# The row term of the cross attention scores: VectorE multiply-and-sum in place of one-column TensorE products

## The reference, cut to what matters

```python
h = _layernorm(x)                      # the normalised row
q = h @ Wq + bq
k_tok, v_tok = h @ Wk + bk, h @ Wv + bv
k_ext, v_ext = ctx @ Wk + bk, ctx @ Wv + bv
s_self = jnp.einsum('bsh,bsh->bs', q, k_tok)[..., None]
s_ext = jnp.einsum('bsh,beh->bse', q, k_ext)
probs = softmax(concatenate([s_self, s_ext], axis=-1))
out = probs[..., :1] * v_tok + jnp.einsum('bse,beh->bsh', probs[..., 1:], v_ext)
x = x + out
```

## Time and profile before

| | |
|---|---|
| median of three runs | 2739.05 us |
| span of the profiled execution | 2732.5 us |
| median less span | 6.55 us |
| TensorE matmuls, busy | 2354.2 us, 86% |
| VectorE, busy | 1869.3 us, 68% |
| ScalarE, busy | 1643.3 us, 60% |
| GpSimd, busy | 1352.9 us, 50% |

### The profile page before, as it was taken

The page is one execution under the profiler, slowest core; times in us unless marked ns, Lnnn a source line. Parts: engine busy times, 40 slices in busy tenths (PEclk is TensorE's granted clock), DMA queues, the critical chain, the costliest instruction groups (busy, mean ns, idle before and its releaser), DMA issues. The chain is left out here.

```text
span 2732.5 us, 49486 instructions
## 1 busy us (share of the span) xinstructions
PE 2354.2 (86%) x16048; PEld 1842.8 (67%) x16048; DVE 1869.3 (68%) x4490; ACT 1643.3 (60%) x3283; POOL 1352.9 (50%) x1313
## 2 busy tenths in 40 slices
PE   5999999669999958999999999986999898599881
PEld 3667676559999835565665656654787777599881
DVE  3888888545656437777777777772777777477783
ACT  3777777545555426776766767663444343388883
POOL 4777777453334255455454545521556565202556
PEclk9999999779999978999999999996999999799996
DMA  2222222152222001111111111113233433355896
GB/s 62 73 67 74 70 71 66 40 168 73 86 65 66 18 29 32 42 39 43 41 41 42 38 42 39 33 39 127 86 117 121 137 124 107 128 160 181 275 279 199
DMA packets 236524, 241.65 MB, mean 88 GB/s; under 512 B 36926, under 2 KB 222528, under 8 KB 236144
## 3 DMA queue, kind: packets, MB, share of 16 engines
q1 hardware_dynamic: 214704, 192.11, 23.0%
q0 software_dynamic: 20480, 46.39, 5.3%
q10 hardware_dynamic: 1088, 0.00, 0.0%
HBM read 132.78 MB, written 101.25 MB: 86 GB/s over the span
## 5 line engine op out<-in xcount | busy, mean ns | idle before, releaser
L1554 DVE TENSOR_REDUCE f_nm<-f_raw 128x4 f32<-128x1024 f32 x256 | 312.8, 1222 | 107.5 <-PE f_raw L1667 104.6
L1390 POOL TENSOR_TENSOR f_hm<-f_hm,f_mhalf 128x64 f32<-128x64 f32 x32 | 366.4, 11449 | 2.7
L1459 ACT ACTIVATE f_PT<-f_sco 128x1024 f32<-128x1024 f32 x256 | 262.2, 1024 | 99.1 <-PE f_sco L1684 98.7
L2399 POOL DMA_INDIRECT d_pick<-expert_out,e_out_slots x128 | 133.2, 1041 | 221.7 <-DMA expert_out<-d_eo 135.7
L916 ACT ACTIVATE b_hT<-b_H,b_b1r 128x512 f32<-128x512 f32 x128 | 88.4, 691 | 162.4 <-PE b_H L1046 147.0
L1684 PE MATMUL f_sco<-f_q4T,f_k4T 64*128 64x256 f32 x1024 | 130.9, 336 | 51.0 <-DMA f_q4T<-f_nmT 36.6
L1925 POOL DMA_INDIRECT expert_in<-g_xm,e_slots x128 | 129.8, 1014 | 40.2 <-issue 37.0
L677 PE MATMUL a_bank<-a_w,a_xnT 128*128 128x512 f32 x256 | 127.1, 621 | 21.9 <-ACT a_xnT L394 21.9
L1061 PE MATMUL b_O<-b_w2l,b_hTh 128*128 128x256 f32 x512 | 145.9, 285 | 0.0
L1061 PE MATMUL b_O<-b_w2h,b_hTh 128*128 128x256 f32 x512 | 144.7, 283 | 0.0
L1061 PE MATMUL b_O<-b_w2h,b_hTl 128*128 128x256 f32 x512 | 143.6, 280 | 0.0
(11 more groups left out here) (368 smaller groups left out, 7722.3 us busy)
## 6 DMA issues: line engine op xcount, KB each, us to landing
e_xs<-expert_in SPq DMA_DIRECT2D x85, 256.0 KB, 3.3
expert_out<-d_eo SPq DMA_DIRECT2D x85, 256.0 KB, 2.5
x_scratch<-a_x SPq DMA_DIRECT2D x64, 256.0 KB, 3.1
b_w<-in_L_ffn_W_dram SPq DMA_DIRECT2D x16, 1024.0 KB, 5.7
a_x<-in_x_dram SPq DMA_DIRECT2D x32, 256.0 KB, 3.8
a_cx<-in_ctx_dram SPq DMA_DIRECT2D x32, 256.0 KB, 3.4
f_x<-x_scratch SPq DMA_DIRECT2D x32, 256.0 KB, 2.7
f_q4T<-f_nmT SPq DMA_DIRECT2D x128, 64.0 KB, 2.3
```

The costliest lines, as they stand in the source:

```text
L1390: g.tensor_tensor(hm[b % 2][:, :], hm[b % 2][:, :], mhalf[:, :], ALU.pow).then_inc(hroot, 1)
L1459: s.activation(PT[n % 3][:, t, :, :], heads(SCO), ACT.Exp, scale=float(DH) ** -0.5).then_inc(probs_ready, 1)
L1554: v.tensor_reduce(nm[:, t, g * HG:(g + 1) * HG], heads(RAW), AX.X, ALU.max, negate=True)\
L2399: g.indirect_dma_start(pick[b % GR][:, t, c, :], None, ex.eo_d[k], bass.IndirectOffsetOnAxis(ap=ex.out_slots[:, b, t, c:c + 1], axis=0), b ...
```

## The change

The row term is no longer a TensorE product. A new VectorE part, "pre r" (`row_term`), multiplies the normalised row by `wr`, now held as a full row of 256 values on every partition, and sums the product over the columns by the accumulator output of the instruction; it does so once per tile, one round ahead of its use, between "mix mix" and "sco exp". Its result has two buffers. `score_max` reads it there and adds bq·bk inside the two small steps, so the two L2033 instructions go. One wait (`r2_ready`) is added ahead of the first small step, and waits for `xn_ready` and the previous `r2_ready` ahead of the new part. In the attention pass `wr` is made by two 256-column products in place of four one-column ones, and its copy is 256 columns wide instead of 2.

```diff
-        self.wqk, self.g0, self.wr, self.r0 = ..., sb("wr", [P, C]), sb("r0", [P, 1])
+        self.wqk, self.g0, self.wr, self.r0 = ..., sb("wr", [P, D]), sb("r0", [P, 1])
...
-                s.activation(w.wr[:, :], Y[:, C:2 * C], ACT.Copy).then_inc(pro_sb, 1)
+                s.activation(w.wr[:, :], halves(Y)[:, 1, :], ACT.Copy).then_inc(pro_sb, 1)
...
-                    for c in range(C):
-                        t_.matmul(Y[:, C + m:C + m + 1], wqT[:, c, cols], w.bkT[:, c:c + 1], start=c == 0, stop=c == C - 1)
+                for c in range(C):
+                    t_.matmul(halves(Y)[:, 1, :], w.bkT[:, c:c + 1].broadcast_to([P, P]), wqT[:, c, :],
+                              start=c == 0, stop=c == C - 1)
...
-            "mix mix", "sco exp", "pre T", ...
+            "mix mix", "pre r", "sco exp", "pre T", ...
...
                 for t, bank in enumerate((S0, S1)):
                     v.tensor_reduce(m2[:, t:t + 1], bank[:, 0:S + 1], AX.X, ALU.max).then_inc(gate_step, 1)
-                    v.tensor_scalar(r2[:, t:t + 1], bank[:, S + 2:S + 3], r0[:, 0:1], None, ALU.add).then_inc(gate_step, 1)
-                small[0] += 4
+                small[0] += 2
                 dve.wait_ge(gate_step, small[0])
-                v.tensor_tensor(m2[:, :], m2[:, :], r2[:, :], ALU.add).then_inc(gate_step, 1)
+                dve.wait_ge(r2_ready, b + 1)
+                v.scalar_tensor_tensor(m2[:, :], r2[b % 2][:, :], r0[:, 0:1], m2[:, :], ALU.add, ALU.add).then_inc(gate_step, 1)
                 small[0] += 1
                 dve.wait_ge(gate_step, small[0])
-                v.tensor_tensor(nb2[:, :], r2[:, :], m2[:, :], ALU.subtract).then_inc(nb2_ready, 1)
+                v.scalar_tensor_tensor(nb2[:, :], r2[b % 2][:, :], r0[:, 0:1], m2[:, :], ALU.add, ALU.subtract)\
+                    .then_inc(nb2_ready, 1)
+
+            def row_term(b):
+                dve.wait_ge(xn_ready, b + 1)
+                if b:
+                    dve.wait_ge(r2_ready, b)
+                for t in range(T):
+                    last = v.scalar_tensor_tensor(r2_terms[:, t, :], xn[b % 2][:, t, :], 1.0, wr[:, :], ALU.mult, ALU.mult,
+                                                  accum_out=r2[b % 2][:, t:t + 1])
+                last.then_inc(r2_ready, 1)
...
-                for t, bank in enumerate((S0, S1)):
-                    for c in range(C):
-                        t_.matmul(bank[:, S + 2:S + 3], xnT[b % 2][:, c, t * P:(t + 1) * P], wr[:, c:c + 1],
-                                  start=c == 0, stop=c == C - 1)
                 pe.wait_ge(gx_ready, b + 1)
```

More of the change, by code:

```diff
@@ L1090, in __init__ @@
         self.wq_in = [sb("wq_in0", [P, C, D]), sb("wq_in1", [P, C, D])]
-        self.wqk, self.g0, self.wr, self.r0 = sb("wqk", [P, C, D]), sb("g0", [P, C]), sb("wr", [P, C]), sb("r0", [P, 1])
+        self.wqk, self.g0, self.wr, self.r0 = sb("wqk", [P, C, D]), sb("g0", [P, C]), sb("wr", [P, D]), sb("r0", [P, 1])
         self.count = 14
@@ L1756, in cross_pass @@
         pe2, peT = sb("pe2", [P, T, S + 1]), sbn("peT", 2, [P, T, S])
-        m2, nb2, r2 = sb("m2", [P, T]), sb("nb2", [P, T]), sb("r2", [P, T])
+        m2, nb2 = sb("m2", [P, T]), sb("nb2", [P, T])
+        r2, r2_terms = sbn("r2", 2, [P, T]), sb("r2_terms", [P, T, D])
         den2, rden2 = sb("den2", [P, T]), sbn("rden2", 2, [P, T])
@@ L1783, in cross_pass @@
         g_psum, g_ready, gx_step, gx_ready = sem("g_psum"), sem("g_ready"), sem("gx_step"), sem("gx_ready")
+        r2_ready = sem("r2_ready")
         s2_psum, nb2_ready, p2_ready, inverted, own_ready = [sem(n) for n in ("s2_psum", "nb2_ready", "p2_ready", "inverted", "own_ready")]
@@ L1800, in cross_pass @@
             "sco gx", "pre stats", "pre cxT", "gate norm", "part0 high", "sco scores", "gate T", "file rows", "pre norm",
-            "mix mix", "sco exp", "pre T", "sco expT", "mix T", "gate logits", "mix cross", "pre g", "part1 low", "gate ranks")
+            "mix mix", "pre r", "sco exp", "pre T", "sco expT", "mix T", "gate logits", "mix cross", "pre g", "part1 low", "gate ranks")
         PIECES, FIRST = 2 * NE, B // 4
@@ L2178, in _ @@
             slots({"part1 low": split_weights,
-                   "pre stats": stats, "pre norm": norm, "sco scores": score_max, "sco expT": invert, "mix mix": add_mix,
+                   "pre stats": stats, "pre norm": norm, "pre r": row_term, "sco scores": score_max, "sco expT": invert, "mix mix": add_mix,
                    "mix cross": add_cross, "gate norm": norm3, "gate logits": gates, "gate ranks": queue})
```

## The result

The changed kernel takes 2747.01 us (median of 12 runs, 2740.58 to 2756.32) against 2740.02 (12 runs beside it, 2725.05 to 2743.43): ratio 1.0034, 95% interval [1.0018, 1.0051]. A ratio is always that of a kernel to the kernel before, measured beside it, and the brackets behind it are its 95% interval. The forecast was 2732.0 us in a range of 2725 to 2745. The kernel became slower: the difference is small, but the interval lies above 1. The profiled spans go the same way: 2732.5 before, 2748.9 after.

A forecast was written before the change was run, and what follows sets the result against it. GpSimd's chain up to the own score, then VectorE's from the maximum, was taken to bound the cross-pass round. Net 0.22 us over 32 batches saves 7.0 us: span 2725.5, plus 6.55 gives 2732.0 us, range 2725 to 2745.

The forecast's parts named there:

- The folded weights: Making the wider wr, once: eight one-column matmuls become four of 256 columns, the copy grows; below 1 us, taken as 0.
- Rival 3: Cross pass: idle time ahead of the own score drops TensorE's clock, 1.1 us a drop; about 2750 us, chance 0.10.
- The products go: Cross pass, TensorE ahead of the own score: 8 loads, 1.08 us a round, become about 0.92 us idle; gain 0.
- Two small VectorE instructions go: Cross pass, score_max: first maximum to bias falls from 1.24 to 0.99 us, saving 0.25 us a round.
- I cost that at 0: score_max's two small steps becoming scalar-tensor-tensor forms on two columns: no added cost, each still 0.16 us.
- the extra wait: Ahead of score_max's first small step: already fulfilled, handling costs 0.03 us a round (bounds 0 and 0.11).
- Does the rest follow?: Cross pass behind score_max: TensorE's 0.47 us wait ahead of the mix transposes lets the round shorten by the whole 0.22 us.
- The new VectorE part: Cross pass, two multiply-and-sum instructions: 1.1 us (0.88 to 1.35) fits in 1.60 us of room, cost 0.
- The extra wait at its upper bound: Rival "same": the added score_max wait costs 0.11 us, leaving 0 to 4 us gain; about 2737 us, chance 0.30.
- TensorE as the bound: Cross pass: removing the products saves 1.08 us a round, 35 us in all; about 2697 us, chance 0.02.
- Idle takes the clock: Cross pass: 1.3 us without matmuls drops TensorE's clock, 1.1 us a drop; about 2750 us, chance 0.10.
- Row term not hidden: Cross pass: the new VectorE pair takes 2.76 us against 1.60 of room; about 2769 us, chance 0.05.

The follow-up runs named there:

- e1: The changed kernel with 32 unused bytes per partition behind wr (1024 in all); 2728.11 us, ratio 0.997 to the kernel before.
- e2: The kernel before with 992 unused bytes per partition behind wr, no instruction changed; 2759.4 us, ratio 1.0098.
- e16: The kernel before with 32 unused bytes behind wr, and 96 ahead of and 32 behind q4T and nmT each; ratio 1.0001.
- e14: The kernel before with 64 unused bytes per partition behind wr; 2744.6 us, ratio 1.0025.
- e15: The kernel before with 128 unused bytes per partition behind wr; ratio 1.0016.
- e18: The changed kernel with 32 unused bytes ahead of nmT alone and 224 behind it; 2730.72 us, ratio 0.9976 to the kernel before.
- e8: e1 with the removed one-column products put back on TensorE, their result unused; 2731.01 us, ratio 0.998 to the kernel before.
- e17: The kernel before with 32 unused bytes ahead of q4T and 96 behind it; ratio 1.006.
- e7: e1 with bq·bk added a round early by its own instruction, and plain two-operand steps in score_max; 2730.98 us, ratio 0.9968 to the kernel before.
- e11: e1 with GpSimd's indirect DMAs made to wait until the normalised row is written; 2732.31 us, ratio 0.9979 to the kernel before.
- e10: e1 with both the early bq·bk of e7 and the DMA wait of e11; 2725.24 us, ratio 0.9956 to the kernel before.
- e9: e1 with the row term made three times, the extra sums unused; 2739.77 us, ratio 1.0004 to the kernel before.

## Why the prediction was wrong

*The folded weights* is the step that failed: "Both ways below 1 us in all; I take 0". I priced the instructions that make the wider `wr` and not the tile itself. It stands early in the allocation, and its 992 bytes took nmT off a multiple of 256 in another pass. By the ratios this is 1.0034 - 0.997 = 0.64% of 2739, about 17.5 us; between the profiles of after and e1 it is 24.0 us of attention pass. To the kernel before the same 992 bytes cost 1.0% (e2). Neither my range nor a rival held it. Rival 3 names nearly the measured time (2750), but that is luck: it was wrong about how, since the granted clock of the cross pass is 0.95 after and 0.93 before.

How the 24 us come about: from the sixth round on, 0.27 us more in each of 26 rounds (26.2 for 25.9 us undisturbed) is about 7 us; 0.25 of the 0.27 are TensorE's longer wait. In the same rounds 22 instead of 12 hold a stretch at half clock, of 1.1 us each: 10 x 1.1 = 11 us. The first rounds give 3 us more and the end of the pass nearly 4. That the longer wait brings the stretches at half clock is not shown. Of the rounds that begin between 1100 and 1780 us they are in 21 in after and 11 in before, but in 16 in e16, with a wait of 1.32 us, and in 5 in e14, with 1.46. What brings them, and why e14 and e15 with nearly the same packets as the others lose only 4 to 7 us, is open. A single profile is a weak witness here: e18's, with packets of 33 ns and 14 rounds with such a stretch, some of them longer, has an attention pass of 923.6 us and belongs to one of its slowest runs (2743.54), while its median stands by e1's.

*The products go*: right in the plain round (e8), 0.93 us of idle time against 0.92. The pass gained 9.6 and not 7.0 although each round gained less than forecast, but 5.7 of the 9.6 us are also the difference between before and e17, in which the cross pass is unchanged. So the nearness of 9.6 to 7.0 is luck.

*Two small VectorE instructions go*: the maximum pair 0.76 as forecast; "I cost that at 0" was wrong, each of the two steps takes 0.22 instead of 0.16. This is why a plain round gained 0.13 and not 0.22: 0.25 - 2 x 0.06 = 0.13, and the extra wait, for which I had taken off 0.03, isn't seen (2217.05 to 2217.09, the plain gap of 0.04). It isn't the second operator that costs: the two-operator step L2126 of after, whose scalar is a constant, takes 0.16 on four columns, and the one-operator step L2056 of e7, which reads r0 from memory, takes 0.23 on two. The rows had a sign of it, since L2033, which reads r0 as well, took 0.21 for one column.

*Does the rest follow?*: the whole of what ScalarE gained, yes. But the margin that I gave for it, the 0.47 us wait of TensorE ahead of the mix transposes, says nothing about the chain over the normalised row. There only 0.06 us of the gain reached the mix sum, and the round did not yet wait for that chain. The row's hold behind GpSimd's indirect DMA did not cost the forecast anything (without it the period of e11 is still 12.78), but it takes what a further gain at the bias would give (e7, e10). The Trainium skill (SBUF — State Buffer, Who interferes with whom) says that VectorE's tensor_scalar can run in a mode that takes a port pair shared with GpSimd, and that then whichever engine issued first keeps the pair for its whole instruction. The trace agrees as far as the row isn't done before the DMA's instruction in plain rounds: 0.73, 0.82 and 0.94 us for the row where the DMA has 0.28, 0.42 and 0.53 us left at its start (the first of these isn't held: without the DMA the row takes 0.73 as well, e11). It differs where 0.61 us and over are left: there the row starts second and ends first, so GpSimd doesn't keep the pair for the whole of this instruction.

*The new VectorE part*: right, hidden. The pair takes 0.77 (forecast 1.1, bounds 0.88 to 1.35), below my lower bound, which came from L562's least, 478 ns. L562 and L2072 (0.48) read their scalar from memory and L2050 has the constant 1.0; the 0.06 us between them are those of the small steps, so this may be the reason. The Trainium skill's rule of half throughput (Vector Engine (DVE) Microarchitecture Reference, Points that are easy to get wrong) is not borne out: L2050 takes 0.42 us for 256 columns from two SBUF tensors, 0.35 from start to start, against 0.48 and 0.40 for L2072 with one source in PSUM.

*Rivals.* The extra wait at its upper bound: out, by the gap of 0.04; its 0 to 4 us in the cross pass hold the 3.9 us found against e17, but by another cause. TensorE as the bound: out, by e8. Idle takes the clock: out, granted clock 1.00 from 2000 to 2050 us. Row term not hidden: out, by e9.

## What to carry to other kernels

- One and the same cross pass, down to the instruction, took 477 us in eight profiles and 471 to 473 in four others.
